# Second layer's expert weights: loaded whole and split inside the expert stage, instead of kept split in DRAM

## What is computed

```
scores  = sigmoid(x @ router.T)                # 16 experts in 4 groups of 4
groups  = the 2 best groups of a token (sum of a group's two best scores + bias)
chosen  = the 4 best experts within those groups
combine = 2.5 * score / sum(chosen scores)
for e in range(16):
    y = (silu(x @ gate[e].T) * (x @ up[e].T)) @ down[e].T
    out += combine[:, e] * y
h = h + out                                    # x is the layernorm of h
```

## Time and profile before

| | us |
|---|---|
| median of 3 runs (lowest, highest) | 1833.39 (1832.42, 1834.61) |
| the profiled execution's own time | 1829.42 |
| its span, first to last instruction | 1827.6 |
| PE busy | 1639.9 (90%) |
| DVE busy | 1105.9 (61%) |
| ACT busy | 732.1 (40%) |
| POOL busy | 385.6 (21%) |

### The profile page before, as it was taken

How to read it: one execution, slowest core, us unless ns; L and a number is a source line. 1 busy time by engine, 2 the same in 40 slices (tenths; PEclk the granted TensorE clock), 3 DMA queues, 4 the chain that set the end, 5 groups by cost and what they waited for, 6 DMA issues and landing times. The chain is left out here.

```text
span 1827.6 us, 40838 instructions
## 1 busy us (share of the span) xinstructions
PE 1639.9 (90%) x15224; PEld 1424.5 (78%) x15224; DVE 1105.9 (61%) x2342; ACT 732.1 (40%) x1224; POOL 385.6 (21%) x314
## 2 busy tenths in 40 slices
PE   7979999999999877999996898888579999999994
PEld 6867888888788756888885676666479989998994
DVE  5645547545545668776676677777646456447452
ACT  4424344434334342222223666666223333333331
POOL 4042110111010013100112333333033232124031
PEclk9999999999999998999998899999569999999997
DMA  7214220120120011000000000000723223223222
GB/s 249 104 58 164 78 87 16 64 100 20 49 81 2 2 36 45 18 9 9 1 0 5 1 2 2 1 0 2 275 81 100 83 83 99 76 80 116 85 88 70
DMA packets 62608, 111.51 MB, mean 61 GB/s; under 512 B 7552, under 2 KB 43776, under 8 KB 61568
## 3 DMA queue, kind: packets, MB, share of 16 engines
q1 hardware_dynamic: 51712, 85.21, 13.7%
q0 software_dynamic: 7872, 23.60, 3.9%
q10 hardware_dynamic: 2880, 0.63, 0.2%
HBM read 62.10 MB, written 47.32 MB: 60 GB/s over the span
## 5 line engine op out<-in xcount | busy, mean ns | idle before, releaser
L1163 DVE SCALAR_TENSOR_TENSOR e_gated<-e_gated,e_share,e_p_gu 128x128 f32<-128x128 f32 x320 | 96.9, 344 | 191.0 <-ACT e_gated L1087 186.1
L113 PE MATMUL e_p_gu<-e_w_hi,e_xt_hi 128*128 x640 | 184.1, 288 | 0.0
L113 PE MATMUL e_p_gu<-e_w_hi,e_xt_lo 128*128 x640 | 183.5, 287 | 0.0
L113 PE MATMUL e_p_gu<-e_w_lo,e_xt_hi 128*128 x640 | 183.4, 287 | 0.0
L1087 ACT ACTIVATE e_gated<-e_p_gu 128x256 f32<-128x256 f32 x160 | 61.3, 384 | 260.6 <-PE e_p_gu L113 260.6
L113 PEld LDWEIGHTS e_p_gu<-e_w_hi,e_xt_lo 128*128 128x128 f32 x640 | 124.9, 195 | 0.0
L113 PEld LDWEIGHTS e_p_gu<-e_w_lo,e_xt_hi 128*128 128x128 f32 x640 | 124.8, 195 | 0.0
L113 PEld LDWEIGHTS e_p_gu<-e_w_hi,e_xt_hi 128*128 128x128 f32 x640 | 124.7, 195 | 0.0
L113 PE MATMUL e_p_y<-e_w_hi,e_hid_hi 128*128 x320 | 108.0, 338 | 15.4 <-issue 14.9
L1063 POOL DMA_INDIRECT e_xn<-results,e_row_of x64 | 65.4, 1022 | 234.2 <-issue 176.0
L113 PE MATMUL a_J<-a_xt_hi,w_qk_hi 128*128 128x512 f32 x256 | 107.0, 418 | 8.2 <-DVE a_xt_lo L1709 6.2
(11 more groups left out here) (322 smaller groups left out, 4786.5 us busy)
## 6 DMA issues: line engine op xcount, KB each, us to landing
e_moved<-rows SPq DMA_DIRECT2D x40, 272.0 KB, 2.9
pa_x<-in_x SPq DMA_DIRECT2D x7, 1536.0 KB, 6.6
results<-e_y SPq DMA_DIRECT2D x40, 256.0 KB, 2.1
rows<-a_zero SPq DMA_DIRECT2D x8, 1088.0 KB, 6.0
w_qk_in<-in_we SPq DMA_DIRECT2D x16, 384.0 KB, 5.9
we_parts<-w_qk_in SPq DMA_DIRECT2D x16, 384.0 KB, 2.3
we_parts<-a_e_lo SPq DMA_DIRECT2D x16, 384.0 KB, 2.6
e_w_hi<-we_parts SPq DMA_DIRECT2D x4, 1536.0 KB, 17.0
```

The lines of the kernel that those rows point to most:

```text
L113: mm = eng.matmul(out, lhs[a], rhs[b], start=start and n == 0, stop=stop and n == len(terms) - 1, skip_group_check=skip)
L1163: last = dve.scalar_tensor_tensor(gated[h % 2][:, b, :], gated[h % 2][:, b, :], share[x % 2][:, b, j:j + 1], up[:, b, :], ALU.mult, ALU.mult)
```

## The change

In `attention0_phase` the splitting of experts is taken out, on POOL and on SP, with its buffer `e_lo` (3 KB of each partition) and four semaphores. SP writes the zeros in single blocks of 128 rows (80 DMAs in place of 12), two or three behind each of the 32 quarter tiles of the attention scores. The DRAM array `we_parts` goes.

In `grouped_phase` SP loads the unsplit weights into the place of the low part, in eight DMAs of two experts (768 KB each) with a semaphore each. ACT copies them, rounded, to the high part, two experts (128x1536) an instruction: one ahead of the end of each of steps 0 to 2, and the other five at step 3, behind the sigmoid. POOL subtracts the high part in place, eight instructions of 128x1536, behind its constants and ahead of its first scatter. PE waits for the eighth subtraction where it waited for the loads.

```diff
@@ grouped_phase, SP
-            for first in range(0, experts, 4):
-                for part in range(2):
-                    sp.dma_start(w[part][:, first * WCOLS:(first + 4) * WCOLS]..., d["we_parts"][part, first:first + 4]...).then_inc(w_here, 16)
+            for n in range(experts // 2):
+                sp.dma_start(of_experts(w[1], n).bitcast(F32).rearrange("p (a n) -> p a n", n=WCOLS),
+                             d["we"][2 * n:2 * n + 2].rearrange("a p n -> p a n")).then_inc(w_here[n], 16)
@@ POOL, behind the constants, ahead of scatter(0)
+            for n in range(experts // 2):
+                pool.wait_ge(w_hi, n + 1)
+                pool.tensor_tensor(of_experts(w[1], n), of_experts(w[1], n).bitcast(F32), of_experts(w[0], n).bitcast(F32), ALU.subtract)\
+                    .then_inc(w_split, 1)
@@ ACT
+            def weights_high(n):
+                act.wait_ge(w_here[n], 16)
+                act.copy(of_experts(w[0], n), of_experts(w[1], n).bitcast(F32)).then_inc(w_hi, 1)
...
+                due = experts // 2 if s >= flow.last_unit[flow.last_own[0]] else s + 1
+                for n in range(rounded, due):
+                    weights_high(n)
+                rounded = max(rounded, due)
@@ PE
-                    pe.wait_ge(w_here, 16 * 2 * (experts // 4))
+                    pe.wait_ge(w_split, experts // 2)
@@ attention0_phase, SP
-            sp.wait_ge(e_free, 1)
-            for e in range(SPLIT_EXPERTS):
-                ...
-                sp.dma_start(e_in, d["we"][e]).then_inc(e_here, 16)
-                for part, have in ((0, e_hi), (1, e_lo[:])):
-                    sp.wait_ge(e_split, 2 * e + 1 + part)
-                    sp.dma_start(d["we_parts"][part, e], have.bitcast(F32)).then_inc(e_stored, 16)
-                ...
+            sp.wait_ge(zeroed, 1)
+            images = CH * TILES
+            for g in range(images):
+                sp.wait_ge(s_out, g + 1)
+                for c, first in blank[g * len(blank) // images:(g + 1) * len(blank) // images]:
+                    sp.dma_start(d["rows"][c][first * P:(first + 1) * P], zero[:]).then_inc(filled, 16)
@@ attention0_phase, POOL
-            def split_expert(e):
-                ...
-                pool.tensor_copy(e_hi, e_in).then_inc(e_split, 1)
-                hold(pool, e_split, 2 * e + 1)
-                pool.tensor_tensor(e_lo[:], e_in, e_hi.bitcast(F32), ALU.subtract).then_inc(e_split, 1)
-                for e in range(per_tile):
-                    split_expert(per_tile * t + e)
```

More of the change, by code:

```diff
@@ L63 @@
 E0, E1 = 8, 16
-SPLIT_EXPERTS = E1
 GROUPS, GROUP_K = 4, 2
@@ L957, in grouped_phase @@
         norm = core.norm
-        consts, w_here = sem("consts"), sem("w_here")
+        consts, w_here, w_hi, w_split = sem("consts"), [sem(f"w_here{n}") for n in range(experts // 2)], sem("w_hi_done"), sem("w_split")
         xn_done, turned, xt_hi, xt_lo, projected = (sem(n) for n in ("xn_done", "turned", "xt_hi_done", "xt_lo_done", "projected"))
@@ L977, in own_block, with of_experts @@
             return chunks[c][0] + 2 * j
+        def of_experts(part, n):
+            return part[:, 2 * n * WCOLS:(2 * n + 2) * WCOLS]
         combine_at = {}
@@ L986, in _ @@
         def _(sp):
-            for first in range(0, experts, 4):
-                for part in range(2):
-                    sp.dma_start(w[part][:, first * WCOLS:(first + 4) * WCOLS].bitcast(F32).rearrange("p (a n) -> p a n", n=WCOLS),
-                                 d["we_parts"][part, first:first + 4].rearrange("a p n -> p a n")).then_inc(w_here, 16)
+            for n in range(experts // 2):
+                sp.dma_start(of_experts(w[1], n).bitcast(F32).rearrange("p (a n) -> p a n", n=WCOLS),
+                             d["we"][2 * n:2 * n + 2].rearrange("a p n -> p a n")).then_inc(w_here[n], 16)
             def load(x):
@@ L1102, in result @@
                 act.copy(y[x % STORES][:].rearrange("p b n -> p (b n)"), p_y[x % 2][:]).then_inc(y_out, 1)
+            def weights_high(n):
+                act.wait_ge(w_here[n], 16)
+                act.copy(of_experts(w[0], n), of_experts(w[1], n).bitcast(F32)).then_inc(w_hi, 1)
             for i in flow.turns(-1):
                 turned_high(i)
+            rounded = 0
             for s in range(total):
@@ L1528, in attention0_phase @@
         st = sb("st", [P, CH, DVE_BN])
-        e_lo, zero = sb("e_lo", [P, WCOLS], F32R), sb("zero", [P, ROW])
-        e_in, e_hi = w_in[0][:, 0:WCOLS], w_in[1][:, 0:WCOLS].bitcast(F32R)
+        zero = sb("zero", [P, ROW])
         wr_in = [sb(f"wr_in{i}", [P, KD, n]) for i, n in enumerate((E0, E1))]
@@ L1534, in attention0_phase @@
         norm = core.norm
-        e_free, e_here, e_split, e_stored, filled, zeroed, r_here, r_hi = (
-            sem(n) for n in ("e_free", "e_here", "e_split", "e_stored", "filled", "zeroed", "r_here", "r_hi"))
-        blank = [(c, first, min(first + 8, rows.shape[0] // P)) for c, rows in enumerate(d["rows"]) for first in range(0, rows.shape[0] // P, 8)]
+        filled, zeroed, r_here, r_hi = (sem(n) for n in ("filled", "zeroed", "r_here", "r_hi"))
+        blank = [(c, first) for c, rows in enumerate(d["rows"]) for first in range(rows.shape[0] // P)]
         w_here, w_split = [sem("w_here0"), sem("w_here1")], sem("w_split")
@@ L1564, in _ @@
         def _(sp):
-            sp.wait_ge(e_free, 1)
-            for e in range(SPLIT_EXPERTS):
-                if e > 0:
-                    sp.wait_ge(e_split, 2 * e)
-                sp.dma_start(e_in, d["we"][e]).then_inc(e_here, 16)
-                for part, have in ((0, e_hi), (1, e_lo[:])):
-                    sp.wait_ge(e_split, 2 * e + 1 + part)
-                    sp.dma_start(d["we_parts"][part, e], have.bitcast(F32)).then_inc(e_stored, 16)
[L1573 to L1576, removed]
+            sp.wait_ge(zeroed, 1)
[4 more added lines that the diff above has]
+                    sp.dma_start(d["rows"][c][first * P:(first + 1) * P], zero[:]).then_inc(filled, 16)
             sp.wait_ge(filled, 16 * len(blank))
@@ L1582, in _ @@
             split_pieces(pool, w_in, w_vo, d["wa0"][4:8], 4, w_here, w_split)
-            pool.wait_ge(zeroed, 1)
-            pool.wait_ge(w_split, 8)
-            pool.nop(nofuse=True).then_inc(e_free, 1)
-            def split_expert(e):
-                hold(pool, e_here, 16 * e + 16)
-                if not is_first(e):
-                    hold(pool, e_stored, 32 * e)
-                pool.tensor_copy(e_hi, e_in).then_inc(e_split, 1)
-                hold(pool, e_split, 2 * e + 1)
-                pool.tensor_tensor(e_lo[:], e_in, e_hi.bitcast(F32), ALU.subtract).then_inc(e_split, 1)
             first = core.h[:, 0:CH, :]
@@ L1603, in _ @@
                 pool.tensor_tensor(core.wr[i][1][:], wr_in[i][:], core.wr[i][0][:].bitcast(F32), ALU.subtract)
-            per_tile = SPLIT_EXPERTS // TILES
-            for e in range(per_tile):
-                split_expert(e)
             with pool.Fori(1, TILES) as t:
@@ L2472 @@
     dram = {k[3:]: nc.dram_tensor(k, v.shape, F32, kind="ExternalInput").ap() for k, v in arrays.items()}
-    dram["we_parts"] = nc.dram_tensor("we_parts", (2, SPLIT_EXPERTS, P, WCOLS), F32).ap()
     rooms = [most_blocks((high - low) * P, GROUP_K, GROUPS) * P for low, high in CHUNKS]
```

## The result

The changed kernel takes 1854.65 us (median of 10 runs, 1845.08 to 1858.16); the kernel before, run beside it on the same chip, 1835.54 us (10 runs). The measured ratio is 1.0096, 95% interval 1.0073 to 1.0118: 17.6 us more, 13.4 to 21.7 (the two medians as they stand lie 19.1 apart). The forecast was +23.1 us on the scale of the medians, above that interval. The profiled execution took 1850.74 us with a span of 1848.9 us, 21.3 above the span of before.

A forecast was written before the change was run, and what follows sets the result against it. PE bounds the last phase's bulk, whose start waits on DVE's routing, POOL's scatters and two transfers. Profiled 1829.42 + 23.6 - 0.5 = 1852.5 us, or 1856.5 us on the medians' scale; 8 in 10: 1845 to 1862.

The forecast's parts named there:

- main step: Last phase: POOL's subtractions and DVE's routing take turns at the shared SBUF ports, making `row_of` 23.6 us late.
- Ahead of the routing: Last phase, steps 0 to 3: the first three subtractions hold DVE's normalisation, delaying the routing's start by 5.8 us.
- In the routing: Last phase: five subtractions in turn with DVE, 3.51 + 0.25 us each, add the rest of the +23.6 us.
- the straight line through 512 and 1024 elements: POOL's subtraction priced at 2.17 ns an element, so 3.51 us for 1536 elements.
- Attention 0's relief: Attention 0: removing the splitting saves only time POOL takes from DVE, -0.5 us, bounds 0 and -2.
- "faster" rival: Attention 0: lifting the lock of 16 subtractions, 30.2 us, outweighs the +23.6, giving 1826.8 us; chance 0.03.
- Loads and copies: Last phase: halved loads land ahead of their copies and ACT's copies of 1.48 us fit its idle time; nothing.

The follow-up runs named there:

- Experiment 1: Changed kernel without POOL's eight subtractions, loads and ACT's copies kept, low part left unsplit: 1911.86 us, ratio 0.9936 to the kernel before.
- experiment 4: Changed kernel with sixteen POOL subtractions of one expert instead of eight of two: 1928.35 us, ratio 1.0026 to the kernel before.
- Experiment 6: Changed kernel with no POOL subtractions; POOL waits ahead of its scatters for 16 copies on ACT: 1829.90 us, ratio 0.9982 to the kernel before.
- experiments 10: Kernel before, POOL's splitting in attention 0 kept, its 48 transfers cut to one load, unsplit weights loaded twice in the last phase: ratio 0.9962.
- 11: Kernel before, all 48 transfers of the splitting kept, POOL only signalling, unsplit weights loaded twice in the last phase: ratio 0.9966.
- experiment 2: Changed kernel with the eight subtractions on DVE, behind the routing (steps 4 to 6 and 8): 1916.98 us, ratio 0.9969 to the kernel before.
- Experiment 9: Against experiment 2, three of DVE's subtractions moved from the ends of steps 4 to 6 to steps 0 to 2: 1922.69 us, ratio 0.9982 to before.

## Why the prediction came out as it did

Its main step held, name by name: the eight subtractions and the routing in turn, the last five without a gap, links of 3.3 to 3.5 us and then of 0.2, `row_of` late, everything behind it at the old distances (505.7 us from `row_of` to the end, against 504.9). Experiment 1 shows that the subtractions are the cause, 4 that a link lasts as long as the POOL instruction beside it, 6 that POOL's queue isn't it.

- **Ahead of the routing: +5.75 forecast, +4.5 measured** (line 1204 at 23.0 us behind the mark, line 1188 at 18.5). PE's transposes were back at 1307.20, not 1307.9: the first two subtractions took 6.87 us where I had 7.35. And I let the third one hold DVE and ACT's sigmoid more than it did: the sigmoid ended at 1313.9, not 1314.4.
- **In the routing: +17.8 forecast, +15.9 measured** (28.4 us from its first link to `row_of`, against 12.5). The five subtractions ran in 16.94 us where I had 18.5. I had put 0.25 us for a DVE link between each two of them, 1.0 us in all, and there is no gap; a subtraction takes 3.42 us, not 3.51, so the straight line through 512 and 1024 elements was 3% high. And DVE passed three links before the fourth subtraction started at 1315.33, and five beside the five: eight rather than five, worth 0.7 us.
- Together `row_of` is 20.4 us late and the last phase 21.2 us longer, not 23.6. That is 2.4 us of the miss.
- **Attention 0's relief: 0.5 forecast, 3.4 to 4.8 measured.** This step failed. I took the stretching of one DVE line for the whole effect. What that line can't show is the time of the lines beside it and of PE's products while the transfers run, and the count of the "faster" rival (30.2 us of subtractions) showed how much could be there. My bounds, 0 and -2, came from a row that couldn't bound it. The gain that this rival spoke of is there, at a sixth of its size or less; of its mechanism, POOL's hold on DVE, DVE's busy time shows about 1 us. Where the rest comes from is open.
- **Loads and copies: nothing, as forecast.** Loads landed after 6.0 to 14.8 us, copies took 1.48, and the first experiment has `row_of` on time with both.

21.2 - 4.8 is 16.4 us and 21.2 - 3.4 is 17.8, beside the 17.6 measured (13.4 to 21.7). Both misses made the forecast too high, and the difference that I forecast lies above the measured interval. That the time itself, 1854.65, is only 1.9 us from 1856.5 is partly luck: the kernel before took 1835.54 beside it, 2.15 above the 1833.39 from which the forecast counts.

Open is what the kernels on the two slower chips gain beyond this. Those without any split gain 10 to 12 us on before, where the relief accounts for 4.8. The gain isn't attention 0's: experiments 10 and 11 are 7.3 and 6.5 us faster than before where their attention 0 gives 2.0 and 0.5, and experiment 4 is 5.0 us slower where 17.2 (its last phase against the first experiment's) less 4.8 would be 12.4. So some 5 to 8 us of every ratio on these chips have no cause shown. The pauses there differ from run to run, and no profile of before exists to compare. Experiment 6, on a faster chip, misses its sum the same way by 1 us at least.

## What to carry to other kernels

Beside long POOL instructions that read two SBUF arrays, count a chain of short DVE instructions whose inputs lie in SBUF as one link for each POOL instruction, whatever a link takes alone; it is the sum of POOL's times that goes on the path. Links that read PSUM (lines 1153 and 1168) went through unhindered. Or give such work to DVE, which did the same subtraction in half the time: in experiment 2 the last phase is 7.2 us longer than without any subtraction, where POOL's cost 21.2 in the profiles of before and after. Experiment 9 shows that it then has to be over when PE resumes. The ratios of experiment 2 and of the changed kernel (0.9969, 1.0096) come from different chips and don't measure that gain. And where a piece of background work is taken out of a phase, compare the phase's length over several profiles before pricing it from one line.

## What the hardware showed beside that

The two engines disturb each other both ways: a scatter that POOL issues in 0.98 us takes 1.36 to 1.96 beside a subtraction of 1.75 us on DVE. A link that met no subtraction took its 0.19 to 0.28 us, right between stretched instructions too (lines 1204 to 1206 of the kernel after), so there is no lasting slowdown, only the wait. And the same program takes 1834 us on one chip and 1924 on two others; in the profiles taken on those two the difference lies in the last phase, where the pauses are.
